# Row maxima crossed over in two halves, and both bias additions moved off GpSimd

## The chip, the cores and the metric

The kernel runs on one core of a Trainium2 chip. The metric is the device time of one execution in microseconds, the median of several runs. TensorE (PE), VectorE (DVE), ScalarE (ACT), GpSimd (POOL) and the queue of SyncE (SP), which here only issues DMAs, run beside one another and meet at semaphores. Each executes its own instructions strictly in program order.

## The reference

A pre-norm transformer block on x of shape (16, 512, 256), float32: banded attention with 16 heads of 16, then a mixture of 8 experts with the two best per token. Cut to what matters:

```python
half = w // 2                                   # w from the data, at most 120
q, k, v = heads(x @ Wq + bq), heads(x @ Wk + bk), heads(x @ Wv + bv)
scores = where(|i - j| <= half, q @ k.T / 4, -1e30)
out = (softmax(scores) @ v) @ W_o               # per head
x = x + out @ Wfc + bfc                         # first residual

gating = softmax(ln(x) @ Wg + bg)               # 8 experts, 2 best
h = silu((x W1[e] + b1[e]) * (x W3[e] + b3[e])) # x here is ln(x)
mixed = sum over the 2 best of gate * (h @ W2[e] + b2[e])
x = x + mixed @ Wf + bf                         # second residual
```

## The kernel before

**Three programs follow one another.** The setup (0 to 48.6 us) scales the weights and folds W_o into Wfc (`wc`) and bv into bfc (`bfc_row`). The attention (48.6 to about 848 us) works batch by batch and, on the way, splits the experts' weights into two float16 halves. The expert stage (from 849 us) walks over 68 tiles of 256 routed tokens.

**Attention.** A step i of the outer loop (i = -1 to 17) has 16 rounds n. The softmax of batch i is made in these rounds: in round n PE writes the scores of one window of four head pairs to `p_exp` (`score_for_exp`), ACT takes the exponentials (`exps`, line 830), and two rounds later PE weighs the values with them (`weigh_values`, line 1322). There is one `p_exp`, so PE's next scores wait for ACT's exponentials. The row maxima that the softmax needs are made a step earlier and three rounds ahead: PE writes the same scores to `p_max` (`score_for_max`, line 1281/1288), DVE reduces them (`row_max`, line 1020). There is one `p_max` too. Rounds 0 to 7 are one half of the head pairs (gk = 0), rounds 8 to 15 the other (gk = 1).

**The crossing of the maxima.** When all 16 maxima of batch i+1 exist, in round 13 of step i, PE transposes them (line 1330), ACT copies the negated result to `m_rows` (line 838), and SP issues four DMAs (line 622) that put them as an extra row into `qs`, so that the matmul of the scores subtracts them. The first `score_for_exp` of step i+1 waits for these DMAs (`s_mrow`).

**Jobs in the shared banks.** Other products of PE (values V, transposes T and G, output D, projections QK, ranks R, maxima M) take turns in two PSUM banks `p_sh`; `JOB_SLOTS` gives each its round. A job waits until the one two places before it has been read out of the same bank. The order in a step is V V T T D D QK QK QK QK G G R M G G.

**Around a step's end.** On GpSimd a step runs through: `residual_bias` (line 718, adds `bfc_row` to the batch's 512x256 input), a hold until DVE's `turn_back`, `low_rows` (732), four indirect scatters (704), `note`, the subtractions `split_qk` (687), in odd steps `low_weights` (714), four more scatters, a hold, `residual_out` (line 728, adds `bf_row` to the batch's 512x256 result), `norm` (675, 682: the scale of the layer norm of a later batch). ACT in round 0 of a step does: exps, `gate_exp` (906, of DVE's logits, 1067), `norm` (789, waits for GpSimd's 682), `scaled_values` (822). In odd steps it also scales weights in rounds 1, 4 and 5 (`scaled_weights`), in even ones it takes squares in rounds 2, 4 and 5. SP stores a finished batch (line 628) after `residual_out`. DVE adds the projected attention to the input (`residual`, line 1055) in rounds 5 and 6.

**Expert stage.** Per tile PE multiplies (lines 1563, 1575), ACT applies b1 and silu (1602, 1607), DVE multiplies and splits (1655, 1662, 1664) and takes the result with b2 (`take_result`, 1670). ACT then copies the token numbers (1618) and multiplies the result with the gate (`weighted`, 1619), and GpSimd adds it to the output by an indirect DMA (1700) after a small instruction that marks the turn (`tick`, 1699).

## Time and profile before

| | |
|---|---|
| runs | 1398.17, 1404.14, 1406.64 us; median 1404.14 |
| span of the profiled execution | 1408.7 us (its own time; 4.6 us above the median) |
| busy share | PE 86%, PE weight loads 63%, DVE 66%, ACT 59%, POOL 49% |
| setup, 0 to 48.6 us | PE busy 26.8 us |
| attention, first part and steps to 802 us | 753 us, PE busy 631 us |
| end of attention and routing, 802 to 853 us | 51 us, PE busy 10.7 us |
| expert stage, 853 to the end | 555.7 us, PE busy 538.5 us |

A busy PE is not a PE at its peak: its clock has two levels, 1.2 and 2.4 GHz, and the granted share is given for each stretch (1.00 is 2.4 GHz all the time).

### The profile page before, as it was taken

The page shows a single profiled execution, that of the slowest core. Times are in us where ns is not written, and L with a number is a line of the kernel's source. Part 1 is how long each engine was busy: PE and PEld are TensorE (multiplying, and loading weights), DVE is VectorE, ACT ScalarE, POOL GpSimd, SP SyncE. Part 2 cuts the span into 40 slices and gives each one's busy share as a digit, 9 for nine tenths or more (in the row PEclk, how much of TensorE's full clock was granted, in tenths as well). Part 3 has the DMA queues.
Part 4 walks back from the last instruction along what each step waited for, and adds up shares of the span by engine and source line. Part 5 has one row for each costly group of instructions (what it writes and reads, how often), then busy time and mean ns, then how long its engine had stood idle before and what let it go on. Part 6 is the DMA issues. An engine that isn't in the chain of part 4 may idle for free. (4 is left out here: it accounts for less than half of the span.)

```text
span 1408.7 us, 46473 instructions
## 1 busy us (share of the span) xinstructions
PE 1206.9 (86%) x18157; PEld 887.4 (63%) x18157; DVE 930.1 (66%) x1999; ACT 825.3 (59%) x1464; POOL 686.9 (49%) x683
## 2 busy tenths in 40 slices
PE   4699888898878888888777717999999999999996
PEld 3455555455544555555554416888888888888885
DVE  7245777687687677776876444666666666666664
ACT  1357767677667667686756413555555555555553
POOL 3122334655647446655555761545444454454545
PEclk9899998999999999999978658999999999999998
DMA  5486454654656537455452425465554665654443
GB/s 171 144 223 165 112 160 121 196 141 134 183 134 188 150 95 223 128 145 158 131 157 66 151 91 114 65 123 96 98 122 68 123 125 70 126 66 69 62 70 46
DMA packets 209963, 176.47 MB, mean 125 GB/s; under 512 B 114427, under 2 KB 174459, under 8 KB 209803
## 3 DMA queue, kind: packets, MB, share of 16 engines
q1 hardware_dynamic: 152458, 116.86, 32.8%
q0 software_dynamic: 25728, 34.17, 13.8%
q10 hardware_dynamic: 31616, 23.19, 6.1%
q8 instruction: 114, 1.87, 0.6%
q14 instruction: 47, 0.38, 0.1%
HBM read 66.95 MB, written 89.89 MB: 111 GB/s over the span
## 5 line engine op out<-in xcount | busy, mean ns | idle before, releaser
L1020 DVE TENSOR_REDUCE mx<-p_max 128x4 f32<-128x496 f32 (+1 forms) x248 | 212.8, 858 | 144.6 <-PE p_max L1288 142.8
L830 ACT ACTIVATE probs<-p_exp,unscale 128x736 f32<-128x736 f32 (+1 forms) x256 | 210.2, 821 | 138.2 <-PE p_exp L1288 125.0
L1563 PE MATMUL p_h<-xt_parts,w_hi 128*128 128x256 f16 x1824 | 273.8, 273 | 3.8 <-DVE xt_parts L1651 3.8
L1655 DVE SCALAR_TENSOR_TENSOR t<-p_h,b,t 128x256 f32<-128x256 f32 x272 | 130.9, 484 | 162.7 <-ACT t L1602 159.1
L1700 POOL DMA_INDIRECT out<-yw,tokens x136 | 212.0, 1558 | 28.2 <-POOL tick L1699 18.5
L1699 POOL TENSOR_TENSOR tick<-tick 128x1 f32<-128x1 f32 x136 | 82.9, 610 | 268.6 <-ACT yw L1619 268.6
L1602 ACT ACTIVATE t<-p_h,b,undo 128x256 f32<-128x256 f32 x272 | 148.2, 558 | 89.4 <-PE p_h L1563 85.4
L1563 PEld LDWEIGHTS p_h<-xt_parts,w_hi 128*128 128x128 f16 x1824 | 178.1, 98 | 25.5 <-DVE t L1655 5.1
L1563 PE MATMUL p_h<-xt_parts,w_lo 128*128 128x256 f16 x912 | 174.0, 273 | 0.0
L687 POOL TENSOR_TENSOR qk_lo<-qf,qk_hi 128x512 f16<-128x512 f32 x64 | 76.5, 1199 | 149.8 <-ACT qk_hi L814 149.6
L1281 PE MATMUL p_exp<-mask,ident_bf 64*64 64x368 bf16 (+1 forms) x1056 | 90.9, 334 | 65.3 <-ACT probs L830 43.5
L1322 PE MATMUL p_out<-probs,v 64*32 64x184 f32 (+1 forms) x4096 | 144.6, 341 | 2.3 <-DVE out_t L1033 1.5
L704 POOL DMA_INDIRECT routed<-rows,slots x128 | 126.9, 991 | 37.3 <-issue 35.5
L1607 ACT ACTIVATE hf<-t 128x512 f32<-128x512 f32 x136 | 85.7, 630 | 78.7 <-DVE t L1655 78.6
L1575 PE MATMUL p_y<-w_hi,h_hi 128*128 128x256 f16 x456 | 124.3, 273 | 1.2 <-DVE y L1670 1.2
L1575 PE MATMUL p_y<-w_lo,h_hi 128*128 128x256 f16 x456 | 124.3, 273 | 0.0
L1575 PE MATMUL p_y<-w_hi,h_lo 128*128 128x256 f16 x456 | 124.3, 273 | 0.0
L1281 PE MATMUL p_max<-mask,ident_bf 64*64 64x248 bf16 (+1 forms) x992 | 86.4, 338 | 30.3 <-DVE mx L1020 30.1
L1664 DVE SCALAR_TENSOR_TENSOR h_lo<-hf,h_scale,h_hi 128x512 f16<-128x512 f32 x136 | 102.2, 752 | 10.2
L1563 PEld LDWEIGHTS p_h<-xt_parts,w_lo 128*128 128x128 f16 x912 | 89.2, 98 | 10.5
L732 POOL TENSOR_TENSOR rows<-x2n,rows 128x1024 f16<-128x1024 f32 x16 | 33.0, 2064 | 124.9 <-DVE att L1047 124.9
L1618 ACT ACTIVATE tokens<-words 128x2 uint16<-128x2 uint16 x136 | 26.6, 196 | 107.0 <-DVE y L1670 79.6
(266 smaller groups left out, 2603.2 us busy)
## 6 DMA issues: line engine op xcount, KB each, us to landing
qk_dram<-qk_hi SPq DMA_DIRECT2D x128, 128.0 KB
qs<-qk_dram SPq DMA_DIRECT2D x64, 192.0 KB, 3.9
ks<-qk_dram SPq DMA_DIRECT2D x64, 192.0 KB, 4.3
x_in<-in_x SPq DMA_DIRECT2D x64, 128.0 KB, 2.5
qk_dram<-qk_lo SPq DMA_DIRECT2D x64, 128.0 KB
w_mat<-in_W ACTq DMA_DIRECT2D x32, 256.0 KB
out<-x_sb SPq DMA_DIRECT2D x64, 128.0 KB, 2.2
w_split<-w_first_hi SPq DMA_DIRECT2D x24, 256.0 KB
```

The lines of the kernel that those rows point to most:

```text
L704: nc.gpsimd.indirect_dma_start(out=io["routed"], out_offset=bass.IndirectOffsetOnAxis(ap=slots[b % 3][:, j, t:t + 1], axis=0), in_=rows[b ...
L830: nc.scalar.activation(probs[r % 3][:, :, 0:hi - lo].rearrange("p (e s) w -> p e s w", e=2), p_exp[:, :, 0:2 * WIN].rearrange("p e (s w) - ...
L1020: nc.vector.tensor_reduce(out=maxes, in_=max_buffer(r, p_max, p_exp)[:, :, 0:2 * WIN].rearrange("p e (s w) -> p e s w", s=2)[:, :, :, 0:hi ...
L1281: nc.tensor.matmul(out, keep["ident_bf"][Q * e:Q * e + Q, Q * e:Q * e + Q], keep["mask"][Q * e:Q * e + Q, None, off:off + hi - lo].to_broa ...
L1322: last = nc.tensor.matmul(p_out[32 * g:32 * g + 32, half, lo:hi], v[b % 3][rows_of, k, 4 * gk + g, :], probs[r % 3][rows_of, g, 0:hi - lo] ...
L1563: last = nc.tensor.matmul(p_h[:, m % KC, k, :], w[e][a][:, k, HID * c + P * m:HID * c + P * m + P], xt[:, x, c, :], start=(n == 0 and c == ...
L1575: last = nc.tensor.matmul(p_y[:, b, :], h[a][:, m, P * b:P * b + P], w[e][v][:, 2, D * m:D * m + D], start=(m == 0 and n == 0 and b % 2 == ...
L1602: nc.scalar.activation(t1[m][:], p_h[:, m % KC, 0, :], ACT.Identity, bias=kept["b13"][:, 0, e, m:m + 1], scale=kept["undo"][:, e:e + 1]).t ...
L1607: nc.scalar.activation(hf[q][:], t3[q][:], ACT.Silu).then_inc(s_silu, 1)
L1655: nc.vector.scalar_tensor_tensor(t3[m // 2][:, m % 2, :], p_h[:, m % KC, 1, :], kept["b13"][:, 1, e, m:m + 1], t1[m][:], ALU.add, ALU.mult ...
L1664: nc.vector.scalar_tensor_tensor(h[1][:, 2 * q:2 * q + 2, :], hf[q][:], kept["h_scale"][:, e:e + 1], h[0][:, 2 * q:2 * q + 2, :], ALU.mult ...
L1700: nc.gpsimd.indirect_dma_start(out=io["out"].rearrange("b s d -> (b s) d"), out_offset=bass.IndirectOffsetOnAxis(ap=tokens[:, b, :].bitcas ...
```

## The change

- **Maxima in two halves.** Each half of the head pairs has its own columns in `mx`, its own transpose, ACT copy, four DMAs and semaphore. The first half crosses in round 6 of the step before, the second in round 13. The shared banks get one more job per step: V V T T D D **M** QK QK QK QK G G R M G G. On SP the first half's four DMAs stand ahead of `stage(i + 3, 0)`. `score_for_exp` waits for the first half in round 0 and for the second in round 8.
- **bfc into PSUM.** GpSimd's `residual_bias` is gone. The setup splits the bias into three bfloat16 parts in rows 0 to 2 of `bias3` (rows below zero), and each of the two `output` jobs of a batch starts with a matmul of ones with `bias3` (128 x 512 bfloat16).
- **bf beside the experts.** GpSimd's `residual_out` is gone. `bf_half` holds bf/2, and each of a token's two gated expert results gets it: the gating moves from ACT (`weighted`) to DVE (`weigh`: two scalar_tensor_tensor of 128x256 a tile, after a drain). ACT only copies the token numbers (`take_tokens`), without waiting for the result. SP's `store` waits for the second D job to be read instead of for `residual_out`; DVE's `residual` waits for the second norm of the batch before instead of for `residual_bias`.

```diff
-JOB_SLOTS = {0: ("V", 1, 0), 1: ("V", 1, 1), 2: ("T", 3, 0), 3: ("T", 3, 1), 4: ("D", -1, 0), 5: ("D", -1, 1), 6: ("QK", 3, 0),
-             7: ("QK", 3, 1), 8: ("QK", 3, 2), 9: ("QK", 3, 3), 10: ("G", -1, 0), 11: ("G", -1, 1), 12: ("R", -2, 0), 13: ("M", 1, 0),
-             14: ("G", -1, 2), 15: ("G", -1, 3)}
+V_AT, T_AT, D_AT, QK_AT, G_AT, M_AT = (0, 1), (2, 3), (4, 5), (6, 7, 8, 9), (10, 11), (6, 13)
+STAGES = (("V", 1, V_AT), ("M", 1, M_AT), ("T", 3, T_AT), ("QK", 3, QK_AT), ("D", -1, D_AT), ("G", -1, G_AT + (LOGITS_AT, TURN_AT)),
+          ("R", -2, (RANK_AT,)))
...
-            nc.vector.tensor_tensor(keep["bfc_row"][:], p_set[:, BIAS_BANK, 0:D], keep["bfc_row"][:], ALU.add)
+            nc.vector.tensor_tensor(bias_left[:], p_set[:, BIAS_BANK, 0:D], bfc_row[:], ALU.add)
+            nc.vector.tensor_scalar(keep["bf_half"][:], keep["bf_half"][:], 0.5, None, ALU.mult)
+            dve.drain()
+            for part in range(3):
+                nc.vector.tensor_copy(bias_part[:], bias_left[:])
+                dve.drain()
+                if part == 0:
+                    nc.vector.tensor_scalar(keep["bias3"][:, 0, :], bias_part[:], keep["ident"][:, 0:1], None, ALU.mult)
+                else:
+                    nc.vector.scalar_tensor_tensor(keep["bias3"][:, 0, :], bias_part[:], keep["ident"][:, part:part + 1], keep["bias3"][:, 0, :],
+                                                   ALU.mult, ALU.add)
+                if part < 2:
+                    nc.vector.tensor_tensor(bias_left[:], bias_left[:], bias_part[:], ALU.subtract)
+                dve.drain()
+            nc.vector.tensor_copy(keep["bias3"][:, 1, :], keep["bias3"][:, 0, :])
             dve.drain()
...
+            def store_max(b, gk):
+                taken(sp, s_free, "M", b, gk)
                 for e in range(2):
                     p0 = Q * e + 3 * HD
                     for half in range(2):
+                        pr = HALF * half + 2 * gk
+                        sp.dma_start(qs[b % 2][p0:p0 + 1, pr:pr + 2, :].rearrange("a s (k q) -> a (s k) q", q=Q),
+                                     m_rows[Q // 4 * e:Q // 4 * e + Q // 4, gk, Q * half:Q * half + Q]).then_inc(s_mrow[gk], 16)
             def store(b):
-                sp.wait_ge(s_xo, b + 1)
+                taken(sp, s_free, "D", b, 1)
...
+                if exists(i + 1):
+                    store_max(i + 1, 0)
                 if exists(i + 3):
                     stage(i + 3, 0)
                 if stored_expert(i) is not None:
                     store_low_weights(stored_expert(i))
                 if exists(i + 1):
-                    store_max(i + 1)
+                    store_max(i + 1, 1)
...
-                if exists(i):
-                    residual_bias(i)
...
-                if exists(i - 1):
-                    residual_out(i - 1)
...
             def score_for_exp(b, n):
+                if n % NK == 0:
+                    pe.wait_ge(s_mrow[n // NK], 16 * MROW_DMAS * (b + 1))
                 if n == 0:
-                    pe.wait_ge(s_mrow, 16 * MROW_DMAS * (b + 1))
                     wait(pe, s_mx, ROUNDS)
...
             def output(b, k):
                 bank = shared("D", b, k)
+                nc.tensor.matmul(p_sh[:, bank, :], keep["ones_bf"][:], keep["bias3"][:].rearrange("p t d -> p (t d)"), start=True, stop=False,
+                                 skip_group_check=True)
                 if k == 0:
                     pe.wait_ge(s_att, 2 * b + 2)
...
+            def take_tokens(g):
                 act.wait_ge(s_words, 16 * g + 16)
-                act.wait_ge(s_y, g + 1)
                 for b in range(NB):
                     after(act, s_sc[b], 16 * g)
-                    nc.scalar.activation(tokens[:, b, :], words[:, b, M_TOKEN:M_TOKEN + 2], ACT.Copy)
-                    nc.scalar.activation(yw[:, b, :], y[:, b, :], ACT.Copy,
-                                         scale=words[:, b, M_GATES + 2 * e:M_GATES + 2 * e + 2].bitcast(F32)).then_inc(s_yw, 1)
+                    nc.scalar.activation(tokens[:, b, :], words[:, b, M_TOKEN:M_TOKEN + 2], ACT.Copy).then_inc(s_tok, 1)
...
+            def weigh(e, g):
+                dve.drain()
+                dve.wait_ge(s_words, 16 * g + 16)
+                for b in range(NB):
+                    after(dve, s_sc[b], 16 * g)
+                    nc.vector.scalar_tensor_tensor(yw[:, b, :], y[:, b, :], words[:, b, M_GATES + 2 * e:M_GATES + 2 * e + 2].bitcast(F32),
+                                                   kept["bf_half"][:], ALU.mult, ALU.add).then_inc(s_yw, 1)
...
                 split(e, g, p, 1)
+                if p is not None:
+                    weigh(before, p)
```

## Rows read from the trace of the kernel before

**Rows 1.** Busy time by stage: us, busy of each engine, PEclk, DMA share, GB/s.

```profile
147.00:802.00 655.00, 551.06 (x11861) 330.62 (x11861) 474.14 (x1067) 452.80 (x675) 359.46 (x325) 0.91 0.52 145
853.00:1408.70 555.70, 538.45 (x4896) 479.71 (x4896) 359.03 (x681) 303.67 (x681) 259.21 (x272) 0.99 0.54 91
```

**Rows 2.** Who waited for whom: us in total, times, longest.

```profile
PE p_exp L1281 <- ACT probs L830: 43.5, 60, 1.8
PE p_max L1281 <- DVE mx L1020: 30.1, 32, 4.5
PE p_exp L1281 <- DMA qs<-m_rows: 21.2, 9, 3.8
```

**Rows 3.** Timeline where even steps begin: step 4 (two rows), then step 6.

```profile
280.62 0.20 POOL L682 TENSOR_TENSOR shift<-less,rs 128x4 f32<-128x4 f32 x1 [2.95 <-issue]
285.60 0.87 ACT L830 ACTIVATE probs<-p_exp,unscale 128x736 f32<-128x736 f32 x1
...
360.79 2.88 SPq L622 DMA_DIRECT2D qs<-m_rows  x4
363.37 2.35 POOL L728 TENSOR_TENSOR x_sb<-x_sb,bf_row 128x1024 f32<-128x1024 f32 x1
366.36 0.19 DVE L1067 TENSOR_TENSOR lg<-lg,gm 128x32 f32<-128x32 f32 x1
367.89 0.42 PE L1281 MATMUL p_exp<-mask,ident_bf 64*64 64x248 bf16 x4 [2.94 <-DMA qs<-m_rows]
369.24 0.43 PE L1269 MATMUL p_sh<-wv_hi,xh 128*64 128x128 f16 x4
369.26 2.06 ACT L789 ACTIVATE xn<-x_in,shift,rs 128x256 f32<-128x256 f32 x4
371.94 0.52 PE L1281 MATMUL p_max<-mask,ident_bf 64*64 64x368 bf16 x4
376.25 0.87 ACT L830 ACTIVATE probs<-p_exp,unscale 128x736 f32<-128x736 f32 x1
```

**Rows 4.** Timeline: PE in step 5, start of odd step 7, end of step 13.

```profile
322.77 0.30 PE L1269 MATMUL p_sh<-wv_hi,xh 128*64 128x128 f16 x4
324.23 0.35 PE L1281 MATMUL p_max<-mask,ident_bf 64*64 64x368 bf16 x4
...
404.70 3.04 DVE L1108 TENSOR_TENSOR picked<-one,pos 128x32 f32<-128x32 f32 x1
405.32 2.36 POOL L728 TENSOR_TENSOR x_sb<-x_sb,bf_row 128x1024 f32<-128x1024 f32 x1
409.26 0.35 PE L1281 MATMUL p_max<-mask,ident_bf 64*64 64x368 bf16 x4 [2.46 <-DVE mx L1020]
413.25 2.06 DVE L1067 TENSOR_TENSOR lg<-lg,gm 128x32 f32<-128x32 f32 x1
...
724.05 0.52 PE L1281 MATMUL p_max<-mask,ident_bf 64*64 64x368 bf16 x4 [4.54 <-DVE mx L1020]
```

**Rows 5.** Round 6 of step 4 on PE and DVE.

```profile
296.41 0.60 PE L1256 MATMUL p_sh<-xh,wq_hi 128*128 128x512 f16 x2
296.58 0.68 DVE L1055 TENSOR_TENSOR x_sb<-p_sh,x_in 128x512 f32<-128x512 f32 x1
296.85 0.59 PE L1256 MATMUL p_sh<-xl,wq_hi 128*128 128x512 f16 x2
```

**Rows 6.** Groups by line and form: count, busy us, mean ns, idle before.

```profile
L1330 PE MATMUL p_sh<-ident,mx 128*128 128x128 f32 x16 | 5.2, 326 | 0.7 <-DVE mx L1020 0.7
L1700 POOL DMA_INDIRECT out<-yw,tokens x136 | 212.0, 1558 | 28.2 <-POOL tick L1699 18.5
L474 DVE TENSOR_TENSOR bfc_row<-p,bfc_row 128x256 f32<-128x256 f32 x1 | 0.4, 415 | 0.0
```

**Rows 7.** DVE in one tile of the expert stage (one every 7.86 us).

```profile
1085.59 0.75 DVE L1664 SCALAR_TENSOR_TENSOR h_lo<-hf,h_scale,h_hi 128x512 f16<-128x512 f32 x1
1086.78 1.04 DVE L1655 SCALAR_TENSOR_TENSOR t<-p_h,b,t 128x256 f32<-128x256 f32 x2 [0.44 <-ACT t L1602]
```

More of the change, by code:

```diff
@@ L114, in shared_bank_jobs @@
     for i in range(FIRST_STEP, LAST_STEP + 1):
-        for n in sorted(JOB_SLOTS):
-            stage, ahead, k = JOB_SLOTS[n]
-            if exists(i + ahead):
-                order.append((stage, i + ahead, k))
+        for n in range(ROUNDS):
+            for stage, ahead, rounds in STAGES:
+                if exists(i + ahead):
+                    order.extend((stage, i + ahead, k) for k, at in enumerate(rounds) if at == n)
     return {job: n for n, job in enumerate(order)}
@@ L503, in build_attention @@
         xt2 = sb("xt2", [P, NC, S])
-        m_rows = sb("m_rows", [Q, P], F16)
+        m_rows = sb("m_rows", [Q // 2, 2, P], F16)
         st1, mv1, rs1, var1, less1, shift1 = (keep[n] for n in ("st1", "mv1", "rs1", "var1", "less1", "shift1"))
@@ L549, in build_attention @@
         s_stack = [[sem(f"s_stack{gk}{p}") for p in range(2)] for gk in range(2)]
-        s_mrow = sem("s_mrow")
+        s_mrow = [sem(f"s_mrow{gk}") for gk in range(2)]
         s_x2st, s_scat = sem("s_x2st"), [sem(f"s_scat{p}") for p in range(3)]
-        s_lg, s_ge, s_ch, s_xo = sem("s_lg"), sem("s_ge"), sem("s_ch"), sem("s_xo")
+        s_lg, s_ge, s_ch = sem("s_lg"), sem("s_ge"), sem("s_ch")
         s_mv2, s_rs2, s_x2n = sem("s_mv2"), sem("s_rs2"), sem("s_x2n")
@@ L832, in exps, with maxima @@
                                      ACT.Exp, scale=unscale[:, 3:4]).then_inc(s_pr, 1)
-            def maxima(b):
-                bank, _, full = job("M", b, 0)
+            def maxima(b, gk):
+                bank, _, full = job("M", b, gk)
                 act.wait_ge(s_full[bank], full)
-                wait(act, s_mrow, 16 * MROW_DMAS * b)
-                nc.scalar.activation(m_rows[:], p_sh[0:Q, bank, 0:P], ACT.Copy, scale=-1.0 / M_SCALE).then_inc(s_free[bank], 1)
+                wait(act, s_mrow[gk], 16 * MROW_DMAS * b)
+                nc.scalar.activation(m_rows[:, gk, :], p_sh[0:Q // 2, bank, 0:P], ACT.Copy, scale=-1.0 / M_SCALE).then_inc(s_free[bank], 1)
             def gate_operand(b, c):
@@ L1050, in residual @@
                 if k == 0:
-                    dve.wait_ge(s_res, b + 1)
+                    wait(dve, s_x2n, b)
                     wait(dve, s_x2st, 16 * NT * b)
@@ L1215, in _ @@
                             turn_back(i, 0)
-                    if exists(i - 2) and n == 13:
+                    if exists(i - 2) and n == RANK_AT + 1:
                         place(i - 2)
@@ L1325, in weigh_values, with transpose_max @@
                 last.then_inc(s_pv, 1)
-            def transpose_max(b):
-                bank = shared("M", b, 0)
-                pe.wait_ge(s_mx, ROUNDS * b + ROUNDS)
-                nc.tensor.transpose(p_sh[:, bank, 0:P], mx[:, b % 2, :], keep["ident"][:]).then_inc(s_full[bank], 1)
+            def transpose_max(b, gk):
+                bank = shared("M", b, gk)
+                pe.wait_ge(s_mx, ROUNDS * b + NK * gk + NK)
+                nc.tensor.transpose(p_sh[:, bank, 0:P], mx[:, b % 2, gk, :], keep["ident"][:]).then_inc(s_full[bank], 1)
             def output(b, k):
                 bank = shared("D", b, k)
+                nc.tensor.matmul(p_sh[:, bank, :], keep["ones_bf"][:], keep["bias3"][:].rearrange("p t d -> p (t d)"), start=True, stop=False,
+                                 skip_group_check=True)
                 if k == 0:
@@ L1398, in _ @@
                     if exists(i + 1):
[L1399 to L1402 removed]
+                        if n in V_AT:
+                            values(i + 1, V_AT.index(n))
+                        if n in M_AT:
+                            transpose_max(i + 1, M_AT.index(n))
                     if exists(i + 3):
[L1404 to L1407 removed]
+                        if n in T_AT:
+                            transposes("T", i + 3, T_AT.index(n), xn, s_xn)
+                        if n in QK_AT:
+                            project(i + 3, QK_AT.index(n))
                     if exists(i - 1):
[L1409 to L1413 removed]
+                        if n in D_AT:
+                            output(i - 1, D_AT.index(n))
+                        if n in G_AT:
+                            transposes("G", i - 1, G_AT.index(n), x2n, s_x2n)
+                        if n == LOGITS_AT:
                             gate_logits(i - 1)
[L1415 removed]
+                        if n == TURN_AT:
                             turn_logits(i - 1)
[L1417 removed]
+                    if exists(i - 2) and n == RANK_AT:
                         rank(i - 2)
@@ L1632, in body @@
                 if p is not None:
-                    weighted(before, p)
+                    take_tokens(p)
             at = None
@@ L1683, in body @@
                 split(e, g, p, 1)
+                if p is not None:
+                    weigh(before, p)
             copy_columns(0)
-            take_result(NE - 1, tiles(dve, body))
+            last_tile = tiles(dve, body)
+            take_result(NE - 1, last_tile)
+            weigh(NE - 1, last_tile)
         @block.gpsimd
```

91 lines of the change are left out of this document (35 added, 56 removed).

## The prediction

> **What bounds the kernel now.** I read the time by stage first. In the expert stage PE is busy 538 of 556 us; there only something that reaches PE counts. In the steps from 147 to 802 us PE is busy 551 of 655 us at a granted clock of 0.91, so some 104 us of idling and a share of half-speed work are what a change can win there; DVE (474) and ACT (453) are not far behind PE [rows 1]. Next the list of waits: in the attention PE idles for ACT's exponentials (43.5 us), for DVE's maxima (30.1 us) and for the DMAs that carry the maxima (21.2 us in nine waits, up to 3.8) [rows 2]. Then the timeline, where the steps turn out to come in pairs.
>
> Where an even step begins, PE has finished its three-rounds-ahead scores and stands still for 2.94 us, until the four DMAs issued from 360.79 have landed. It then works at the lower clock level (1.2 GHz): the twelve value products take 2.7 us (369.24 to 371.94) [rows 3], against 1.46 us at 2.4 GHz (322.77 to 324.23) [rows 4]. With the rest of the round, which doubles too, the lower level costs 1.2 to 1.9 us on top of the wait.
>
> Where an odd step begins the wait for the DMAs is missing, because another stall has already eaten it. DVE's `place` multiplies two small SBUF tensors; it starts at 404.70 and ends at 407.74, just after GpSimd's `residual_out` (405.32 to 407.68), though an instruction of that size and kind takes 0.19 us where nothing is in its way (line 1067 in [rows 3]). PE then waits 2.46 us for the row maximum behind it. A little later the subtraction of the logits (line 1067) takes 2.06 us instead of the 0.19 of the step before [rows 3, 4]; it too ends when a GpSimd addition (`residual_bias`) ends, and ACT's whole round 0 waits for it. So both removed GpSimd instructions hold up DVE, and through it PE. The largest case is 4.54 us near 724 us [rows 4], where both ran back to back.
>
> The Trainium skill has this as a rule: in SBUF — State Buffer, section "SBUF: two separate sides", DVE and GpSimd share a port pair under an exclusive lock, taken by a GpSimd instruction or by a DVE instruction with two SBUF inputs, and the loser waits for the whole instruction. The trace agrees (3.04 us instead of twice 0.19 at most), and nothing below needs the rule.
>
> **Part 1: the maxima in halves; what is late next.** The wait of 2.94 us goes entirely: the first half crosses seven rounds before it is needed, the second, which crosses where all of it does now, gets eight more rounds. The question is what follows. At the even start of step 6, PE could write p_exp at 364.95 (367.89 less the wait). ACT's exponentials would end by 365.6, but its next instructions need the logits, ready at 366.55. From there ACT has 0.22 (gates) + 2.06 (norm) + 0.69 + 0.87 + 0.69 (values, exponentials, values), some overlapping by a tenth, and would start the exponentials of round 2 at 371.1 instead of 376.25 [rows 3]: 5.1 us won, wait, clock and all. In step 4 ACT waits in addition for GpSimd's scale at 280.62. Without the 2.36 us of `residual_out` ahead of it that is 278.3, and the same sum gives 282.6 instead of 285.60 [rows 3, 4]: 3.0 us. Those are the two ends; there are six even starts with a large wait (steps 2 to 12). Only step 4 shows the long gap on GpSimd, so I take 4.2 each: 25 us.
>
> **Part 2: GpSimd without the additions.** At an odd start go 2.46 us (PE's wait), 1.9 (the logits) and part of the slow clock, 0.9: 5.2 us, for the four starts of steps 5 to 11 [rows 4]: 21 us. The stall near 724 us gives 4.5 + 1.9 of clock = 6. The small rest (the three short waits of 0.3 to 1.1 us on the DMAs, and the starts of steps 3 and 13, which I take at 2 each) gives 5 to 6. Ends for the odd starts: 2.5 each if ACT alone sets the pace afterwards, 5.2 if not. Together parts 1 and 2 give 25 + 21 + 6 + 5 = 57 us.
>
> **What the change costs in the steps.** PE is without gaps in rounds 4 to 9, so what is added there is on the path.
> - Sixteen more transposes at 0.26 us (one after the other; 0.33 each by the group) [rows 6]: 4 us.
> - Thirty-two bias matmuls of 512 columns. The nearest row is the projection with 512 columns, two in 0.44 us (296.41 to 296.85) [rows 5]: 0.22 each, 7 us. Bounds: 0 if an idle moment hides them, 0.43 each at the lower clock.
> - A new wait. The extra job shifts the turns in the two shared banks: the first projection now needs the bank of the second D job, which DVE reads in `residual`, from 296.58 to 297.26. Before, PE began that projection at 296.41 [rows 5]. With the transpose in between it stands still for about 0.6 us. Queued behind it on PE are all the next scores, and ACT and DVE wait for those. Twelve steps have both jobs: 7 us. Bounds: 0 (hidden where ACT paces the round) and 1.7 us (DVE still behind with its choice of experts when the D job ends), so 0 to 20.
>
> Sum 18 us. Hidden edits: the second ACT copy (0.26 us) falls in a round in which ACT waits for PE; four more DMA issues on SP, 2.9 us per batch by the row [rows 3], delay `stage`, whose data are read most of a step later; `store` now starts without waiting for GpSimd. The Trainium skill speaks against halving: SBUF — State Buffer, "The DMA setup-cost knee", says that a transfer pays about 2 us whatever its size. Here that only counts if someone waits for the halves; if PE still did, sixteen more rounds of issue and landing would cost over 40 us. The rows give the first half most of a step.
>
> **Setup and tail.** DVE ends the setup, and gets ten more instructions of 128x256 there, with drains. The nearest row is 0.415 us [rows 6]; casts and scalings should be shorter. 10 x 0.33 + 0.7 for drains = 4 us, all on the path (3 to 6). At the end of the attention one bias matmul at the lower clock lies on the chain: 0.4 us. `residual_out` is hidden there already.
>
> **Expert stage.** DVE gets two more instructions. The one shown with two SBUF inputs takes 0.75 us for 512 columns; for 256 columns I take 0.48, with the drain about 1.1 us a tile. They follow the second split (ends 1086.34) and the next product is done from 1086.78 [rows 7], so products start 0.6 us later. DVE is busy 66% of the 7.86 us, so 2.6 us per tile are free, and the products of one tile are needed by PE only a tile later. ACT gets 1 us shorter. I cost this at 0.
>
> Profiled execution: 1408.7 - 57 + 18 + 4 + 0.4 = 1374. The median stands 4.6 us below the profiled execution: **1370 us**.
>
> **Rivals.**
> - *ACT takes over.* ACT is busy 453 of 655 us [rows 1] and runs in strict alternation with PE on the single p_exp. If its work only moves into the freed time, half of the 57 us comes: 1370 + 28 = 1398. For: 43.5 us of PE's waits are for ACT [rows 2]. Against: the two starts worked out above already contain ACT's own instructions.
> - *The shared banks cost more.* `residual` stays behind DVE's choice of experts and PE waits 1.7 us in twelve steps: +13, 1383.
> - *The additions on PE vanish in its idle moments:* -18, 1352.
> - *Slower: the gating on DVE.* Place: between the second split and the next product of every tile. Point from which it decides: the pair costs more than the 2.6 us that are free. Price: if each of the two waits out a whole scatter on GpSimd (1.56 us each [rows 6]), the pair costs 4.2 us and 68 tiles pay 1.6 each: +109, about 1480; the first 15 us above the forecast by 0.2 us a tile. Against it: DVE's split, also of two SBUF inputs, lies beside GpSimd's work in every tile and keeps its 0.75 us [rows 7]. By the lock rule of the Trainium skill's SBUF page named above this is the place where the change could hurt; it gives no other number.
> - *The change doesn't do what it says:* PE waits for some other DMA in round 0 or 8, and nothing is won there: about 1395.
>
> **Chances.** Forecast 0.57 (its own range 1358 to 1384), ACT 0.16, banks 0.10, hidden costs 0.08, gating 0.05, the last 0.04. A measurement of this kernel tells about 1% from no change (its runs lie within 8.5 us), so faster means below 1390. The forecast, the banks and the hidden costs lie there, and a part of the ACT case: 0.81. Within 1%: 0.13. Slower: 0.06. The range 1350 to 1398 takes in all but the slow end of the ACT case and the gating.
>
> **What the profile after should show.** No wait of PE for m_rows. Lines 1108 and 1067 on DVE at 0.3 (for two) and 0.2 us everywhere. The PE clock of the steps above 0.95. In round 6 a new wait of PE for DVE's residual, 0.3 to 0.8 us. The setup 4 us longer, the span of the expert stage the same with DVE near 80% and ACT near 45%. Steps of 41 to 42 us instead of 43 to 47. Wrong would be: the clock still falling at the step starts, PE's waits for ACT growing by as much as the others shrink, or gaps on PE in the expert stage.

## The result and the profile after

The changed kernel takes 1396.48 us (median of 5 runs, 1386.79 to 1397.2); the kernel before, beside it, 1401.95. Ratio 0.992, interval 0.9896 to 0.9943. By the medians that is 5.5 us, where 34 were forecast. The profiled execution has a span of 1394.8 us, 13.9 below before. The two profiles aren't alike, though: this one is of the median execution, the one before of an execution some 6 us above its median (its span alone, 1408.7, is 4.6 above it, and in every run here the time is 1.7 to 1.8 us more than the span). Differences to the profile before are too large by about that.

Where did it go? Three time marks divide each trace: the copy of the maxima in the first round 13, the first product of the expert stage, and PE's last instruction. First the timeline of before at these marks, then that of the changed kernel.

```profile
106.51 0.27 ACT L838 ACTIVATE m_rows<-p_sh 64x128 f16<-64x128 f32 x1 [1.38 <-PE p_sh L1330]
853.30 1.04 PE L1563 MATMUL p_h<-xt_parts,w_first_hi 128*128 128x256 f16 x4 [24.38 <-DVE xt_parts L1651]
1397.69 0.27 PE L1575 MATMUL p_y<-w_hi,h_lo 128*128 128x256 f16 x1
```

```profile
111.41 0.27 ACT L845 ACTIVATE m_rows<-p_sh 32x128 f16<-32x128 f32 x1 [1.39 <-PE p_sh L1338]
824.77 1.03 PE L1574 MATMUL p_h<-xt_parts,w_first_hi 128*128 128x256 f16 x4 [24.80 <-DVE xt_parts L1660]
1382.37 0.27 PE L1586 MATMUL p_y<-w_hi,h_lo 128*128 128x256 f16 x1
```

| | before | after | change | forecast |
|---|---|---|---|---|
| to the first round-13 copy ("setup") | 106.5 | 111.4 | +4.9 | +4 |
| from there to the first product of the experts ("steps") | 746.8 | 713.4 | -33.4 (by the medians about -25) | -38.6 |
| from there to PE's last start ("expert stage") | 544.4 | 557.6 | +13.2 | 0 |

With the end behind PE's last instruction the expert stage gives back 14.6 of the 28.5 us won by its start. (By the medians: 5.5 us won in all, 14.6 lost in the expert stage and 4.9 in the setup, so about 25 won in the steps. This is an estimate: it puts the odd 6 us of the profile before into its steps, since the setup and the expert stage of the same code vary by 1 to 3 us only.) Busy time by stage in the changed kernel, against [rows 1] (us, busy of each engine, PEclk, DMA share, GB/s):

```profile
147.00:802.00 655.00, 551.16 (x12061) 334.75 (x12073) 462.37 (x1140) 462.77 (x702) 306.63 (x315) 0.94 0.55 151
853.00:1394.00 541.00, 516.41 (x4675) 457.08 (x4673) 392.77 (x784) 234.60 (x521) 248.38 (x268) 0.99 0.53 87
```

The clock of the steps rose from 0.91 to 0.94. PE's idle times in them sum to 104.4 us after 125.0 (without the wait of 24 us for the first product of the experts), and it is busy 14.2 us less, for all the work added. In the expert stage DVE is at 73% and ACT at 43%, below the forecast 80 and 45: neither engine is full there. But PE has gaps in that stage: it waits 12.7 us in 14 places for DVE's `xt_parts`, after 5.0 us in 6. The list of waits says more, against [rows 2] (us in total, times, longest):

```profile
ACT tokens L1629 <- DMA out<-yw,tokens: 144.9, 81, 6.3
PE p_exp L1288 <- ACT probs L837: 44.2, 57, 2.5
POOL shift L701 <- issue: 24.8, 10, 6.0
DVE yw L1687 <- DMA out<-yw,tokens: 17.0, 22, 3.1
ACT xn L796 <- POOL shift L701: 15.3, 6, 3.9
PE p_max L1288 <- DVE mx L1027: 10.8, 18, 1.5
```

PE's wait for the maxima's DMAs (21.2 us) is gone, its wait for DVE's maxima fell from 30.1 to 10.8. Three waits are new or have grown. ACT's token copy waits 144.9 us for the scatters out of its buffer, where that was 11.2 us before. DVE's gating waits 17.0 us for the same scatters. And ACT's norm waits 15.3 us for GpSimd's scale, 6.2 before. Here is the last of them, where step 6 begins:

```profile
361.46 0.96 POOL L723 DMA_INDIRECT routed<-rows,slots  x1 [0.30 <-issue]
362.43 1.06 POOL L694 TENSOR_TENSOR rs<-var,neg_half 128x4 f32<-128x4 f32 x1
364.48 0.19 DVE L1074 TENSOR_TENSOR lg<-lg,gm 128x32 f32<-128x32 f32 x1
368.28 0.20 POOL L701 TENSOR_TENSOR shift<-less,rs 128x4 f32<-128x4 f32 x1 [4.78 <-issue]
368.51 2.07 ACT L796 ACTIVATE xn<-x_in,shift,rs 128x256 f32<-128x256 f32 x4 [3.57 <-POOL shift L701]
371.97 0.52 PE L1288 MATMUL p_exp<-mask,ident_bf 64*64 64x368 bf16 x4 [2.46 <-ACT probs L837]
372.85 0.88 ACT L837 ACTIVATE probs<-p_exp,unscale 128x736 f32<-128x736 f32 x1 [0.36 <-PE p_exp L1295]
```

DVE's subtraction of the logits is free of GpSimd: 0.19 us. The exponentials of round 2 start 8.2 us after it (372.85 less 364.67). Before that was 9.7 (376.25 less 366.55 [rows 3]); the forecast's own sum gives 4.6. What is missing is ACT's wait of 3.57 us: the scale comes 5.9 us after the last scatter, though the pow ahead of it started at once. `residual_out` had stood in that time; without it GpSimd waits instead.

The wait of the token copy, in a steady tile of the expert stage:

```profile
1061.19 0.20 ACT L1629 ACTIVATE tokens<-words 128x2 uint16<-128x2 uint16 x1
1063.52 0.20 ACT L1629 ACTIVATE tokens<-words 128x2 uint16<-128x2 uint16 x1 [2.12 <-DMA out<-yw,tokens]
1063.76 0.88 DVE L1687 SCALAR_TENSOR_TENSOR yw<-y,words,bf_half 128x256 f32<-128x256 f32 x2 [0.24 <-issue]
1063.87 1.02 ACT L1613 ACTIVATE t<-p_h,b,undo 128x256 f32<-128x256 f32 x2
```

ACT stands 2.12 us ahead of the second token copy, until the scatter of the tile before has left the buffer. Queued behind it are the two `t` of the next tile, which DVE's products need. In a steady tile that still comes in time (7.86 us a tile in both kernels). Where a new expert starts it doesn't. SP then loads the weights of the next expert, and the scatters near it take 6 to 9 us from issue to landing, against 3.8 in a steady tile (in both kernels). One such start:

```profile
997.01 0.42 SPq L1542 DMA_DIRECT2D w_hi<-w_split  x1
1006.27 0.20 ACT L1629 ACTIVATE tokens<-words 128x2 uint16<-128x2 uint16 x1 [4.08 <-DMA out<-yw,tokens]
1006.28 0.48 DVE L1687 SCALAR_TENSOR_TENSOR yw<-y,words,bf_half 128x256 f32<-128x256 f32 x1 [1.65 <-DMA out<-yw,tokens]
1007.82 0.48 DVE L1687 SCALAR_TENSOR_TENSOR yw<-y,words,bf_half 128x256 f32<-128x256 f32 x1 [1.06 <-DMA out<-yw,tokens]
1009.21 0.94 DVE L1664 SCALAR_TENSOR_TENSOR t<-p_h,b,t 128x256 f32<-128x256 f32 x2 [0.90 <-ACT t L1613]
1012.26 0.61 PE L1574 MATMUL p_h<-xt_parts,w_hi 128*128 128x256 f16 x4 [2.48 <-DVE xt_parts L1660]
```

Both engines stand in front of the scatters here, ACT with its token copy and DVE with the gating that was moved to it, and PE runs dry behind them. From one tile's `y` to the next these are 10.99 us, 8.60 at the same place before. Summed over the 67 intervals, the time above 7.86 us is 13.8 us, against 0.5 before, which is the 13.2 us of the table; 10.5 of it lies at the starts of six experts, the rest in single tiles between.

### The profile page after: what moved, and what is told of

Same layout as the page of the kernel before. It is cut to its first block and busy times, and to the rows that moved or that the text cites. A ratio compares the mean times of both kernels' runs of the same rounds, so it can differ in the third digit from the quotient of the medians.

```text
span 1394.8 us, 47057 instructions
## 1 busy us (share of the span) xinstructions
PE 1199.2 (86%) x18189; PEld 883.1 (63%) x18205; DVE 955.1 (68%) x2145; ACT 772.0 (55%) x1344; POOL 605.6 (43%) x651
## 3 DMA queue, kind: packets, MB, share of 16 engines
q0 software_dynamic: 25728, 34.17, 13.8%
## 5 line engine op out<-in xcount | busy, mean ns | idle before, releaser
L1574 PE MATMUL p_h<-xt_parts,w_hi 128*128 128x256 f16 x1824 | 276.0, 274 | 11.2 <-DVE xt_parts L1660 11.1
L1722 POOL DMA_INDIRECT out<-yw,tokens x136 | 218.2, 1605 | 42.9 <-POOL tick L1721 28.2
L1664 DVE SCALAR_TENSOR_TENSOR t<-p_h,b,t 128x256 f32<-128x256 f32 x272 | 126.3, 480 | 106.5 <-ACT t L1613 104.9
L1721 POOL TENSOR_TENSOR tick<-tick 128x1 f32<-128x1 f32 x136 | 69.6, 512 | 275.9 <-DVE yw L1687 275.9
L1613 ACT ACTIVATE t<-p_h,b,undo 128x256 f32<-128x256 f32 x272 | 142.2, 558 | 79.4 <-PE p_h L1574 70.6
L1330 PE MATMUL p_out<-probs,v 64*32 64x184 f32 (+1 forms) x4096 | 139.7, 329 | 4.8 <-issue 3.4
L1288 PE MATMUL p_exp<-mask,ident_bf 64*64 64x368 bf16 (+1 forms) x1056 | 89.0, 325 | 48.1 <-ACT probs L837 44.2
L1629 ACT ACTIVATE tokens<-words 128x2 uint16<-128x2 uint16 x136 | 27.0, 200 | 156.1 <-DMA out<-yw,tokens 144.9
L1673 DVE SCALAR_TENSOR_TENSOR h_lo<-hf,h_scale,h_hi 128x512 f16<-128x512 f32 x136 | 102.2, 751 | 10.1
L1574 PEld LDWEIGHTS p_h<-xt_parts,w_lo 128*128 128x128 f16 x912 | 89.7, 98 | 10.8
L1288 PE MATMUL p_max<-mask,ident_bf 64*64 64x248 bf16 (+1 forms) x992 | 85.9, 335 | 11.7 <-DVE mx L1027 10.8
```

The source lines that it names most:

```text
L1288: nc.tensor.matmul(out, keep["ident_bf"][Q * e:Q * e + Q, Q * e:Q * e + Q], keep["mask"][Q * e:Q * e + Q, None, off:off + hi - lo].to_broa ...
L1330: last = nc.tensor.matmul(p_out[32 * g:32 * g + 32, half, lo:hi], v[b % 3][rows_of, k, 4 * gk + g, :], probs[r % 3][rows_of, g, 0:hi - lo] ...
L1574: last = nc.tensor.matmul(p_h[:, m % KC, k, :], w[e][a][:, k, HID * c + P * m:HID * c + P * m + P], xt[:, x, c, :], start=(n == 0 and c == ...
L1613: nc.scalar.activation(t1[m][:], p_h[:, m % KC, 0, :], ACT.Identity, bias=kept["b13"][:, 0, e, m:m + 1], scale=kept["undo"][:, e:e + 1]).t ...
L1664: nc.vector.scalar_tensor_tensor(t3[m // 2][:, m % 2, :], p_h[:, m % KC, 1, :], kept["b13"][:, 1, e, m:m + 1], t1[m][:], ALU.add, ALU.mult ...
L1673: nc.vector.scalar_tensor_tensor(h[1][:, 2 * q:2 * q + 2, :], hf[q][:], kept["h_scale"][:, e:e + 1], h[0][:, 2 * q:2 * q + 2, :], ALU.mult ...
```

## The experiments

All ratios are to the kernel before on the same chip. Two kinds of chips came up: in the first result, e5 to e8 and e9 to e12 the kernel before takes 1402 to 1404 us, in the others (e1 to e4, e13 to e16, e17, e18) 1454 to 1458. Stage times (in us, cut as above) are from each run's profile, which can be of an execution off the median: e6's is 4.9 us below it, e1's 5.6 below, e12's 8.3 above, e13's 5.4 and e15's 4.7 above.

| run | us | ratio (interval) | setup | steps | expert stage |
|---|---|---|---|---|---|
| e1 | 1453.85 | 0.998 (0.9955 to 1.0006) | 111.5 | 781.4 | 542.6 |
| e2 | 1460.49 | 1.003 (1.0006 to 1.0048) | 110.5 | 788.0 | 547.6 |
| e3 | 1473.14 | 1.011 (1.0071 to 1.0147) | 109.9 | 792.1 | 559.9 |
| e4 | 1461.7 | 1.003 (1.0012 to 1.0056) | 109.4 | 777.7 | 560.4 |
| e5 changed | 1387.63 | 0.988 (0.9825 to 0.9933) | 110.6 | 708.4 | 556.9 |
| e6 | 1400.97 | 0.997 (0.9932 to 1.0001) | 106.0 | 732.0 | 545.4 |
| e7 | 1404.54 | 1.001 (0.998 to 1.0031) | 110.9 | 717.9 | 560.4 |
| e8 | 1401.55 | 0.996 (0.9925 to 0.9987) | 110.6 | 721.4 | 558.3 |
| e9 changed | 1397.55 | 0.994 (0.9912 to 0.9963) | 110.8 | 714.1 | 559.8 |
| e10 | 1376.82 | 0.980 (0.9754 to 0.9843) | 110.1 | 710.3 | 543.8 |
| e11 | 1387.91 | 0.986 (0.9809 to 0.9904) | 110.1 | 706.8 | 560.6 |
| e12 | 1372.08 | 0.974 (0.9679 to 0.979) | 111.1 | 713.3 | 543.1 |
| e13 | 1453.14 | 1.000 (0.9976 to 1.0021) | 111.2 | 783.5 | 549.9 |
| e14 | 1471.42 | 1.015 (1.0099 to 1.0192) | 110.3 | 783.3 | 563.5 |
| e15 | 1466.93 | 1.009 (1.006 to 1.0122) | 109.2 | 791.8 | 557.4 |
| e16 changed | 1469.9 | 1.012 (1.0068 to 1.0166) | 109.0 | 788.2 | 557.9 |
| e17 before | 1463.64 | one run | 106.0 | 799.4 | 545.5 |
| e18 as e13 | 1456.47 | 1.001 (0.9987 to 1.0023) | 109.7 | 781.9 | 547.0 |

**The gating (e1, e10, e2).** e1 and e10 are one kernel on two chips. It puts the gating back on ACT and leaves bf/2 out of the result:

```diff
+                act.wait_ge(s_y, g + 1)
...
+                    nc.scalar.activation(yw[:, b, :], y[:, b, :], ACT.Copy, scale=words[...])   # as in the kernel before
...
-                if p is not None:
-                    weigh(before, p)
```

> The changed kernel with the expert stage of before (ACT gates, waits for the result, copies the tokens after it); bf/2 is then added nowhere, so bf is left out of the result. It measures what the move of the gating costs. Both theories of the expert stage (ACT blocked by its early copy of the tokens; DVE too full with two more instructions) expect the stage back at 555 us instead of 570, no wait of ACT for the scatter beyond some 11 us in all, and the whole 14 to 15 us below the changed kernel: about 1380. If the stage stays at 565 or more, neither holds and something in the attention's end (data in other banks of memory, fill of the regions) is the cause.

> The kernel of the first experiment again (the changed kernel with the gating of the experts' rows left as it was, the experts' last bias left out), now with the changed kernel beside it. If the gating move costs what the expert stages differ by (557 to 560 us with it, 543 to 545 without), it is 13 to 15 us below the changed kernel: ratio 0.978 to 0.982. If that difference comes back somewhere else, the two kernels are equal.

The expert stage returns to 543 to 544 us. With the changed kernel beside it (e9) e10 is 20.7 us faster, 16 of them in that stage. The gating move is the cost, and it doesn't come back elsewhere. e2 keeps it and moves only the token copy:

```diff
+                    nc.vector.tensor_copy(tokens[:, b, :], words[:, b, M_TOKEN:M_TOKEN + 2])    # in DVE's weigh
...
-                    nc.scalar.activation(tokens[:, b, :], words[:, b, M_TOKEN:M_TOKEN + 2], ACT.Copy).then_inc(s_tok, 1)
```

> The changed kernel with the copy of the token numbers moved from ACT to DVE, just ahead of each gating instruction; nothing is left out. Theory 1 (ACT's copy stands ahead of the next tile's first factor in program order and waits there for the landing of the scatter before, 145 us in 81 waits): ACT's wait disappears, the expert stage comes back to 556 to 560 us, total about 1382. Rival (DVE's own added work is what delays the tiles): DVE gets 0.1 to 0.3 us more per tile, so the stage stays at 570 or grows to 575, total 1395 to 1400.

547.6 us (559.9 counted to the very end). e3 and e4, on the same chip, have the changed kernel's expert stage: 559.9 and 560.4. So the copy's place on ACT makes 12 of the 17 us between them and e1. ACT's wait is gone from the list and hasn't moved; DVE meets the same scatters for 5.6 us, less than the 17.0 of its gating in the changed kernel:

```profile
ACT t L1613 <- PE p_h L1574: 188.2, 178, 31.6
DVE tokens L1683 <- DMA out<-yw,tokens: 5.6, 6, 3.0
```

The other 5 us are probably DVE's longer turn, which makes ACT's silu wait 2.7 us behind an expert's start; that was not tried.

**GpSimd's scale (e3, e8, e11).** e3 replaces the drain between pow and scale by a semaphore.

> The changed kernel with the drain between the two GpSimd instructions of the first norm replaced by a semaphore that the first one raises. Theory 2 (a drain on GpSimd also waits for the scatters issued ahead of it, and the removed addition had covered that): the scale of the norm comes 0.2 to 0.5 us after the first instruction instead of up to 4.8 us, ACT's 15.3 us of waits for it go to under 3, the steps become 6 to 12 us shorter, total about 1386. Rival (GpSimd is held by something else there, such as its instruction supply, and the next instruction comes when it comes): same gaps of 3 to 5 us before line 701, total unchanged within 2 us.

The run can't tell: on this chip DVE's variance itself came after the scatters (in step 6 it starts at 373.98, the pow at 374.28), so there was no late scale to cure. In e1, e2 and e16, on chips of that kind and with the drain in place, the scale isn't late either (0.48 us behind the pow in nearly all steps with scatters). The stage times are those of the changed kernel of that kind of chip (e16). e8 instead moves the norm ahead of the second four scatters, e11 the pow of the weight magnitudes as well:

```diff
-                    scatter(i - 3, 1)
                 if exists(i):
                     pool.wait_ge(s_att, 2 * i + 1)
                 if exists(i + 4):
                     norm(i + 4)
+                if split_expert(i) is not None:      # e11 only; e8 leaves it where it was
+                    all_magnitudes(split_expert(i))
+                if exists(i - 3) and i - 3 < PROMPT:
+                    scatter(i - 3, 1)
```

> The changed kernel with GpSimd's pow and scale of the next first norm put ahead of the second four scatters instead of behind them. If it is the four scatters that hold GpSimd (its shift follows the last of them by 5 to 7 us in the even steps), the shift comes some 5 us earlier in the even starts, ACT's wait for it there (3.6 us) goes and with it 2.0 to 2.5 us of PE's gap before p_exp: 12 to 15 us less over six even starts, ratio about 0.99 of the changed kernel beside it. If GpSimd's wait is one for its own instructions or a drain, whatever stands ahead of it, the gap only moves and the time is that of the changed kernel within 0.3 percent.

Half hit. The scale now follows the pow in 0.14 us, ACT's wait for it is gone and PE's waits before p_exp fell from 44.0 (e5) to 30.3 us. But the steps got 13 us longer. e8's timeline of an odd start shows why:

```profile
413.15 0.88 POOL L729 TENSOR_TENSOR w_all<-w_sum,half 128x3 f32<-128x3 f32 x1
414.07 0.17 DVE L1011 TENSOR_SCALAR w_inv<-w_all 128x3 f32<-128x3 f32 x1 [4.82 <-POOL w_all L729]
415.86 0.52 PE L1288 MATMUL p_max<-mask,ident_bf 64*64 64x368 bf16 x4 [3.48 <-DVE mx L1027]
```

The moved scatters stood ahead of the magnitudes, for which DVE waits in front of PE's maxima.

> The changed kernel with GpSimd's pow and scale of the first norm, and behind them the pow of the weight magnitudes, ahead of the second four scatters. The kernel with the norm alone moved lost 14 us of waits before p_exp and won 13 us of waits before p_max, where DVE waited 4.8 us for the magnitudes behind the scatters in the odd starts. If that is all there was against it, this one is 10 to 15 us below the changed kernel (ratio 0.978 to 0.982). If the scatters moved cost in another way (their transfers later, GpSimd's rows late), it is no better than the changed kernel.

9.6 us below the changed kernel beside it (1397.55), just under the 10 to 15 expected, 7.3 in the steps, and the intervals of the two ratios don't meet. Even start in e11: logits done at 360.93, ACT's norm at once, exponentials of round 2 after 6.6 us. So the four scatters ahead of the norm cost 1.6 of the 3.6 us that this start lacked against the forecast (8.2 to 4.6). The other 2.0 are a wait behind the norm that the forecast's sum didn't have: ACT's second `scaled_values` waits 2.22 us for PE's values. Whether it is the drain that waits for the scatters stays open.

**Both (e12, e13, e18).** e12 is e10 with e11's order, and leaves bf/2 out. e13 and e18 are e2 with e11's order and compute everything.

> Both: gating as before, and norm and magnitudes ahead of the scatters. If the two costs lie in different stages and add up, 25 us below the changed kernel: ratio 0.968 to 0.972, the fastest of all. If the starts of the even steps are then bound by something else (ACT's own work), 0.976 to 0.980.

> The changed kernel with the token copy on DVE ahead of the weighing (so ACT waits for no scatter), and norm and magnitudes ahead of the second four scatters; the whole computation is kept. The expert stage falls from 558 to 548 us from its first p_h to PE's last, as in the second experiment, the steps by 3 to 8 us: together 10 to 18 us below the changed kernel, ratio 0.978 to 0.985, faster than both kernels. Rival: the expert stage's gain was of the other chip alone; then only the steps' part remains, 0.986 to 0.99.

> The kernel of e13 again. On a chip where the kernel before takes about 1403 us: the expert stage 548 to 550 us from its first p_h to PE's last, the steps 706 to 711 us, in all 1376 to 1382 us, ratio 0.98 to 0.985. If the two gains don't add up there, 0.986 to 0.99, as the version with the order alone. On a chip where it takes about 1454 us, 1.000 again.

e12 is the fastest run. It is 25.5 us below the changed kernel beside it (e9), the 25 of its first case, though its ratio lies between the two cases. e10 and e11 alone give 20.7 and 9.6, so 4.8 of their sum is missing; with intervals of 5 us and more on each that is no more than noise. Its profile can't settle it. PE's gaps in the steps are 5.5 us shorter there than in e10 (90.6 to 96.1), and PE is busy 9 us longer at a granted clock of 0.91 (from 147 to 802 us), to 0.93 in e10. But it is of the slowest of e12's four executions: 1380.4 us at a clock of 0.939 over the whole run, where the others took 1364.2, 1367.7 and 1376.5 us at 0.956, 0.954 and 0.950. e13 is 16.8 us below the changed kernel beside it (e16), as expected (10 to 18), 8 of it in the expert stage; against the kernel before it is equal, and e18 repeats that (1.001). Neither ran on a chip of the first kind.

**One part alone (e6, e7, e14).** e6 is the kernel before with the halves alone, e7 with the two bias moves alone, e14 is e7 with e11's order.

> The kernel before with the row maxima alone crossed over in two halves; both biases stay on GpSimd, the expert stage is that of before. Theory A (the bias moves pay for themselves nowhere but in the even starts): the m_rows wait of the even starts goes, but ACT then waits there for GpSimd's shift, which comes after the residual bias addition and the scatters, so attention ends some 15 us earlier and the expert stage stays at 544 us from its first p_h to PE's last: ratio 0.985 to 0.99. Theory B (the halves gain the whole of what was forecast for them and the bias moves took it away): attention ends 35 us earlier, ratio 0.975.

> The kernel before with the two bias moves alone; the row maxima stay whole. Theory A: the expert stage is 13 us longer as in the changed kernel (557 us from its first p_h to PE's last), setup 4 to 5 us longer, and the steps gain nothing since the even starts wait for m_rows as before: ratio 1.008 to 1.015. Theory B (the biases were worth something in attention): ratio under 1.003.

> The kernel before with the bias moves alone and norm and magnitudes ahead of the second four scatters; the row maxima cross whole. If the halves are worth what the m_rows waits of PE are (33 us in the kernel with the bias moves alone), this one's steps are 15 us or more above those of the kernel with halves and order (707 us from the first round-13 copy to the first p_h). If the halves are worth little, because a gap in the one place only takes the place of a gap in another, within 8 us of them.

e6 missed: its first product of the experts comes 15.3 us before that of the kernel before, as its theory A has it, but its ratio is 0.997 (0.9932 to 1.0001), not 0.985 to 0.99. Steps by the profiles: halves -14.8 us, biases -28.9, both -32.7 to -38.4 (the changed kernel's three profiles on such chips). All of these have the odd 6 us of the profile before in them, and that of the halves has 4.9 more, since e6's profile is of a short execution. By the medians, with setup and expert stage as profiled, the steps won about 4 us by the halves, 21 by the biases and 25, 33 and 28 by both (first result, e5, e9). So the two parts do add up as far as these runs can tell, and on the chip that ran all three versions both together win more (16.6 us in all, e5) than the parts (3.3 in e6, nothing in e7). In e7 PE's waits for the maxima's DMAs rise:

```profile
PE p_exp L1285 <- ACT probs L834: 33.8, 53, 1.2
PE p_exp L1285 <- DMA qs<-m_rows: 33.4, 16, 4.6
```

yet the steps are only 4 to 10 us longer than with halves too, since its waits for ACT are 10 us shorter. Theory B of e7 hit on the ratio; of theory A the expert stage (560.4 for 557) and the setup came out, but not that the steps gain nothing. What the biases win in the steps, the gating loses in the expert stage. e14's steps (783.3) are those of e13 (783.5), which has halves and order both: on that chip the halves are worth little, by its second case: nothing by the profiles, some 6 us by the medians, for e13's profile is of its slowest execution.

**Terms (e4, e15).** e4 puts the first half's crossing into round 11, so that the first projection needs no bank that DVE still reads. e15 leaves out the 32 bias products, and with them bfc and what bv adds to it.

> The changed kernel with the first half's transpose and copy in round 11 instead of round 6, and its DMAs behind the staging of the projections on SP. Theory 3 (the extra job in round 6 makes PE wait for the residual, 0.58 us in each of twelve steps, on the path): the wait of the projection for DVE's residual is gone, steps 0.5 us shorter, total 5 to 7 us lower, about 1389. Rival (rounds 6 to 9 are paced elsewhere, the wait only moves to the next scores): the wait goes, total within 2 us of the changed kernel.

> The changed kernel without the 32 products that lay the attention's output bias into the shared banks; that bias is left out of the result. By the prediction's term these products cost 0.22 us each, 7 us in all: ratio 0.983 to 0.987 where the changed kernel has 0.988 to 0.992. Rival: they run in time in which PE would have waited for ACT or DVE, and leaving them out gives under 3 us.

In e4 the wait of 0.58 us is gone, and the experts' first product comes at 887.2 us, 10 before e16's. That is another chip, but e1, e2 and e3 ran beside e4 and have the attention of the changed kernel (e3 with its semaphore). Median less the expert stage to the very end is 900.3, 900.6 and 901.0 us in these three and 889.0 in e4. So the crossing in round 6, with its DMAs ahead of `stage`, costs about 11 us on that chip, more than the 5 to 7 expected. e4 moves both the crossing and the order on SP; which of the two it is stays open, and it wasn't run on a chip of the first kind. e15: 3 us below e16, intervals overlapping. The 32 products are busy 13.3 us in the changed kernel of e9 (416 ns each, overlapped), and what leaving them out gave can be told neither from 0 nor from the 7 us forecast.

**The other kind of chip (e5, e9, e16, e17).**

> The changed kernel itself, on the same chip as the runs beside it, as their measure. If all chips treat it alike, its ratio to the kernel before is 0.992 again. The theory that the gain depends on the chip (the chip of the first four experiments ran the kernel before in 1458 us, 56 us above the chip of the blind result) expects a ratio of 1.000 to 1.007 on a chip where the kernel before takes about 1458.

> The changed kernel once more, as the measure of the three beside it: 0.988 to 0.992 of the kernel before on a chip where that takes about 1402 us.

> The changed kernel as the measure of the three beside it: 0.988 to 0.994.

> The kernel before itself, for its trace on another chip. On a chip where it takes about 1455 us: its expert stage is 544 us as on the first chip, and all of the 50 us lie in its steps behind 300 us, where the scatters run. If the change's gain in the steps is lost there because PE's gaps without a cause are the same in both kernels and cover what the change removes, its steps (first round-13 copy to first p_h) take 790 to 800 us, no more than 5 us above those of the changed kernel (788). On a chip where it takes about 1403 us it repeats the trace of before: steps of 745 to 750 us.

The changed kernel wins 0.6 to 1.2% on chips of the first kind and loses 1.2% on one of the second, where e16 missed its expectation altogether. e5 came out at 0.988 where 0.992 was expected, e9 at 0.994, just outside its 0.988 to 0.992. e17's steps (799.4) lie in the 790 to 800 us expected, but 11 above e16's and not at most 5. Stage by stage, setup and expert stage are the same there; the steps are longer, by 53 us in e17 and by 74 us in e16. From 300 to 720 us the changed kernel looks so on a chip of the first kind (e9), then on one of the second (e16):

```profile
300.00:450.00 150.00, 131.29 (x2850) 77.35 (x2834) 109.96 (x270) 113.19 (x172) 78.64 (x79) 0.95 0.61 164
450.00:600.00 150.00, 132.60 (x2871) 80.66 (x2870) 108.91 (x267) 111.59 (x171) 67.91 (x74) 0.95 0.58 155
600.00:720.00 120.00, 102.77 (x2398) 62.98 (x2400) 87.16 (x201) 82.26 (x125) 58.53 (x55) 0.97 0.58 161
```

```profile
300.00:450.00 150.00, 129.02 (x2556) 73.73 (x2555) 97.45 (x242) 101.86 (x153) 63.71 (x69) 0.93 0.51 136
450.00:600.00 150.00, 130.35 (x2553) 75.22 (x2552) 97.52 (x233) 99.15 (x155) 68.98 (x69) 0.90 0.59 158
600.00:720.00 120.00, 103.33 (x2108) 60.41 (x2110) 76.28 (x185) 78.65 (x119) 48.74 (x50) 0.89 0.46 130
```

PE is as busy, but does a tenth fewer matmuls in the time, at a lower clock. The list of waits has entries there (e16) that no trace of the first kind has:

```profile
ACT probs L837 <- remote: 63.8, 24, 4.4
DVE mx L1027 <- remote: 43.5, 13, 4.8
PE p_max L1295 <- issue: 9.1, 15, 1.1
```

On such a chip the change wins 0 to 11 us in the steps (the trace of e17 is of a run 9 us above that chip's other one), too little for setup and expert stage. What makes PE slower there isn't in these traces and stays open.

## Why the prediction was wrong

The forecast was 34 us less, by the medians measured were 5.5, on the first kind of chip. Of the 29 us missing the expert stage has 14.6, the setup 0.9 and the steps about 13 (an estimate, as above). By the spans it is 20.8 us (1374 and 1394.8) and the steps have 5.2, but that counts the odd 6 us of the profile before as won. The prediction took 4.6 us off its span for the same reason, as if every profile stood so far above its median; the changed kernel's doesn't.

- **"Expert stage: I cost this at 0" failed.** The instructions on DVE had the price forecast (0.48 us each) and lay where they were put, and "ACT gets 1 us shorter" is true. The sum looked at busy time and not at the waits in the two queues. Missed was that ACT's token copy, no longer behind its wait for `y`, comes ahead of the scatter that must leave its buffer, and stands there 2.1 us a tile with the next tile's `t` behind it. At a new expert's start, where the scatters land late, DVE's gating waits for them as well. The sign named for this case, gaps on PE in the expert stage, is there (12.7 us, after 5.0). e2 gets 12 of 17 us back by moving the copy, e1 and e10 all by moving the gating.
- **The slower rival had the right engines and the wrong mechanism.** Its rule was that DVE's instructions wait out the scatters on GpSimd. None did: 0.88 us for two. They seldom met: 5 of the 136 lie beside a scatter for more than 0.1 us, and these keep 0.48 us too, as do the 15 of DVE's splits that lie beside one (0.75). The argument against the rival had less to stand on than it says, since in the kernel before none of the 136 splits lies beside a scatter, only beside `tick`. What did cost was the landing of the scatters, for which both engines wait. Where GpSimd's long additions were, the prediction was right: DVE's `picked` took up to 4.61 us before and takes at most 0.255 after. The Trainium skill (SBUF — State Buffer, section "SBUF: two separate sides") says that a GpSimd instruction that reads SBUF and one of DVE with two SBUF inputs shut each other out for a whole instruction; the trace agrees for the additions (4.61 us against 0.255), and the instructions with two SBUF inputs that lie beside a scatter keep their 0.48 and 0.75 us.
- **"I take 4.2 each: 25 us" for the even starts failed too.** The halves were put at 25 - 4 - 7 = 14 us, and e6 has about 4 by the medians; the biases at 32 - 7 = 25, and e7 has about 21. So the steps won about 25 (28 and 33 in e9 and e5) of 38.6, and most of what is missing is the halves'. "Without the 2.36 us of `residual_out` ahead of it" the scale does not come earlier: it comes 5.9 us after the scatters, so as soon as the maxima cross in halves ACT waits there (10.1 us behind 250 us, e6 11.0, with both additions still on GpSimd; e7 none). "Only step 4 shows the long gap on GpSimd" no longer held: the even steps from 4 to 12 have 3.0 to 6.0 us each. e11 gives 7.3 us back. What the rest is isn't shown.
- **Small terms.** The new wait for the residual's bank is 0.58 us in each of twelve steps, 7.0 us as forecast; e4, without the crossing in round 6, won about 11 us on the second kind of chip, so this wait may not be all that the early crossing costs. Setup 4.9 for 4. The bias products' 7 us are neither found nor excluded (e15). The clock of the steps is 0.94, where over 0.95 was forecast.
- **"ACT takes over" (1398) has the number (1396.48), not the cause.** PE's waits for ACT hardly grew: 43.5 to 44.2 us.

## What to carry to other kernels

An instruction that gets rid of a wait moves up in its engine's queue, and meets the next wait on its own buffer with other work behind it; look for that wait even where it cost nothing so far. An instruction taken off an engine gives nothing if that engine would have waited there anyway. Before a part of a change is priced from two profiles, compare both with the medians of their kernels: here one profile 6 us above its median and one 5 below made 15 us of 4. Where two chips differ by 4%, measure a change of 1% on both.

## What was unexpected in the hardware

- The same kernel takes 1402 to 1404 us on some chips and 1454 to 1458 on others, nearly all of it in the steps; the expert stage of the kernel before is 544.4 us on the one and 545.5 on the other.
- GpSimd's pow starts 0.01 us after the last of four scatters, the instruction behind it (with a drain between) only after 4.8 us more; with the scatters behind both, after 0.14 us.
- The spread of one kernel's executions goes with PE's granted clock: e12 took 1364.2 us at 0.956 and 1380.4 at 0.939, e6 1389.2 at 0.950 and 1407.5 at 0.932.
- Where a new expert's weights are loaded, a scatter of 128 rows lands 6 to 9 us after its issue, in a steady tile 3.8.
